# Score chunks of the first head inside the last context tiles of a perceiver layer

## The reference, cut to what matters

```python
q = (x @ wq).reshape(B, L, 16, 128)
k, v = ((x @ w).reshape(B, L, 4, 128) for w in (wk, wv))
k_ctx, v_ctx = ((h_ctx_kv @ w).reshape(B, T, 4, 128) for w in (wk_ctx, wv_ctx))
q, k, k_ctx = rms_norm(q, q_norm_w), rms_norm(k, k_norm_w), rms_norm(k_ctx, k_norm_w)
q, k = rope(q), rope(k)
k_full, v_full = concatenate([k_ctx, k]), concatenate([v_ctx, v])   # T + L = 4352 keys
scores = einsum('blhd,bmhd->bhlm', q, repeat(k_full, 4)) * scale + mask   # own keys causal
out = einsum('bhlm,bmhd->blhd', softmax(scores), repeat(v_full, 4)) @ wo
```

## Time and profile before

| | us |
|---|---|
| median of 3 runs | 1052.37 (1051.82 to 1052.49) |
| profiled execution | 1051.38 |
| its span, first to last instruction | 1049.3 |

### The profile page before, as it was taken

How to read it: one execution, slowest core, us unless ns; L and a number is a source line. 1 busy time by engine, 2 the same in 40 slices (tenths; PEclk the granted TensorE clock), 3 DMA queues, 4 the chain that set the end, 5 groups by cost and what they waited for, 6 DMA issues and landing times.

```text
span 1049.3 us, 15552 instructions
## 1 busy us (share of the span) xinstructions
PE 1035.7 (99%) x5789; PEld 885.7 (84%) x5789; DVE 777.2 (74%) x1661; ACT 602.7 (57%) x1090; POOL 182.4 (17%) x200
## 2 busy tenths in 40 slices
PE   7999999999999999999999999999999999999998
PEld 6888888887888888888888888888886888888887
DVE  5856777648777777777877777877668877777775
ACT  4344434334865566665566666568448466666664
POOL 4643344330000000000000000002202112222221
PEclk9999999999999999999999999999999999999999
DMA  6658675498004240042200431004450376555540
GB/s 235 233 195 286 229 241 173 133 317 293 37 1 139 73 131 1 1 171 81 91 1 1 171 121 56 1 1 182 161 231 1 121 285 214 195 191 183 190 169 21
DMA packets 64155, 145.76 MB, mean 139 GB/s; under 512 B 3888, under 2 KB 42704, under 8 KB 62672
## 3 DMA queue, kind: packets, MB, share of 16 engines
q1 hardware_dynamic: 64080, 144.77, 40.0%
HBM read 108.55 MB, written 36.21 MB: 138 GB/s over the span
## 4 chain that ended last, share of the span: by engine, by line
PE 95%; DVE 2%; ACT 1%; POOL 0%; issue 0%; DMA 0%; ACTq 0%
PE bank L549 18%; PE bank L486 16%; PE bank L592 12%; PE bank L569 11%; PE bank L467 11%; PE bank L847 8%; PE bank L594 6%; PE bank L849 4%; PE bank L649 2%; PE bank L662 1%; PE bank L496 1%; PE bank L780 1%; PE bank L717 1%; DVE e_hl L1192 0%; PE bank L818 0%; PE bank L521 0%
## 5 line engine op out<-in xcount | busy, mean ns | idle before, releaser
L1058 DVE TENSOR_TENSOR pT<-bank,pT 128x512 fp32r<-128x512 f32 x272 | 184.8, 689 | 103.3 <-ACT pT L1485 101.5
L1485 ACT CAST pT<-bank 128x512 fp32r<-128x512 f32 x272 | 156.1, 594 | 142.7 <-PE bank L569 139.5
L592 PE MATMUL bank<-pT,vN 128*128 128x512 f32 (+1 forms) x544 | 225.7, 422 | 0.0
L549 PE MATMUL bank<-kT,qT_hi 128*128 128x512 f32 (+2 forms) x576 | 214.5, 391 | 2.1 <-DVE scores L1002 2.1
L1002 DVE TENSOR_SCALAR_CACHE_REDUCE scores<-bank 128x512 f32<-128x512 f32 x256 | 172.8, 686 | 1.7
L569 PE MATMUL bank<-ident,scores 128*128 128x128 f32 x1072 | 161.3, 272 | 0.4 <-DVE pT L1058 0.3
L1456 ACT ACTIVATE scores<-scores,neg_max 128x1024 f32<-128x1024 f32 (+2 forms) x128 | 154.0, 1203 | 5.7 <-DVE neg_max L1014 5.7
L594 PE MATMUL bank<-pT,vN 128*128 128x256 f32 (+1 forms) x544 | 152.5, 280 | 0.0
L486 PE MATMUL bank<-w_ctx_hi,ctx_hl 128*128 128x512 f32 x512 | 146.0, 398 | 6.5 <-ACT ctx_hl L1365 6.5
L847 PE MATMUL bank<-fT_parts,e_hl 128*128 128x512 f32 x392 | 140.0, 395 | 0.1
L569 PEld LDWEIGHTS bank<-ident,scores 128*128 128x128 f32 x1072 | 127.2, 140 | 12.1 <-DVE pT L1058 1.2
(11 more groups left out here) (224 smaller groups left out, 1563.9 us busy)
## 6 DMA issues: line engine op xcount, KB each, us to landing
e_raw<-in_experts SPq DMA_DIRECT2D x51, 768.0 KB, 4.3
k_spill<-k_stage SPq DMA_DIRECT2D x16, 1024.0 KB, 4.5
v_spill<-v_stage SPq DMA_DIRECT2D x16, 1024.0 KB, 8.4
vN<-v_spill SPq DMA_DIRECT2D x16, 1024.0 KB, 5.2
kT<-k_spill SPq DMA_DIRECT2D x15, 1024.0 KB, 5.3
ctx_raw<-in_ctx SPq DMA_DIRECT2D x15, 512.0 KB, 4.3
w_raw<-in_w_qkv SPq DMA_DIRECT2D x6, 1024.0 KB, 5.0
wo_sb<-in_wo SPq DMA_DIRECT2D x4, 1024.0 KB, 9.5
```

Source lines behind the costliest of these rows:

```text
L549: done = e.matmul(bank[b][:, 0:n], qT[a][:, h, qt * P:(qt + 1) * P], kT[:, w, lo:lo + n], start=m == 0, stop=m == 2)
L592: e.matmul(halves[:, :, q0:L], vN[:, 0, kt, :], ring[:, :, i * L + q0:(i + 1) * L], start=kt == 0, stop=False)
L1058: e.tensor_tensor(ring[:, 1, :], bank[tb][:, :], ring[:, 0, :], ALU.subtract).then_inc(p_lo, 1)
L1485: e.copy(ring[:, 0, :], bank[tb][:, :]).then_inc(p_hi, 1)
```

## The change

- Nine chunks of head 0 move into the last three context tiles, three in each, behind the steps `k` = 0, 1, 2 of `project`, in banks 6 and 7. DVE evicts a tile's three ahead of its other work for the tile.
- Five chunks are left for `second`, in banks 0, 2, 6, 7, 0; three of them go ahead of the transpose of tile 31's keys.
- `ahead` has 4 chunks of head 1 in place of 8; the other 4 follow in the steps of head 0.
- In tile 31 ACT squares the projected keys before it copies the transposed keys of tile 30, and DVE forms the rest of tile 30's keys behind the sum of squares. DVE forms the rest of tile 31's values only after both maxima of head 0. It forms the rest of tile 31's keys behind two evictions.
- SP loads pieces 0, 1 and 2 of the values ahead of the last spill, once all tiles are projected.
- Regions s01 and v change places, so `front` lies over k and s01, and `back` over spare, v, s23 and pt; `chunk_max` moves to region keep.

```diff
+EARLY = 3
...
-        for i, c in enumerate(EARLY_CHUNKS):
-            self.add(0, 0, c, (0, 2, 6, 7)[i % 4])
-        self.first = list(range(len(self.chunks)))
-        for c in EARLY_CHUNKS:
-            self.add(0, 1, c)
-        self.second = list(range(len(self.first), len(self.chunks)))
+        for i, (qt, c) in enumerate([(qt, c) for qt in range(2) for c in EARLY_CHUNKS]):
+            self.add(0, qt, c, (6, 7)[i % 2] if i < EARLY * 3 else (0, 2, 6, 7)[(i - EARLY * 3) % 4])
+        self.first = {NT - EARLY + i: list(range(3 * i, 3 * i + 3)) for i in range(EARLY)}
+        self.second = list(range(3 * EARLY, len(self.chunks)))
...
-        for _ in range(8):
+        for _ in range(4):
             self.ahead.append(self.add(1, *ahead.pop(0)))
...
-        sizes = dict(keep=12288, k=34816, v=34816, spare=16096, s01=34816, s23=34816, pt=12288, q=32768)
+        sizes = dict(keep=12288, k=34816, s01=34816, spare=16096, v=34816, s23=34816, pt=12288, q=32768)
...
PE, project(i):
+                    if i in plan.first and k < KD - 1:
+                        in_turns([plan.first[i][k]], None)
...
PE, after the tiles:
-            for s in plan.first:
-                in_turns([s], None)
+            in_turns(plan.second[:3], None)
             turn(NT - 1)
-            for s in plan.second + plan.third + plan.ahead:
+            for s in plan.second[3:] + plan.third + plan.ahead:
                 in_turns([s], None)
...
DVE, in the loop over tiles:
+                if i in plan.first:
+                    for s in plan.first[i]:
+                        evict(s)
-                if i >= 1:
+                if 1 <= i < NT - 1:
                     rest_of_k(i - 1)
                 after(i)
...
DVE, after(i), in place of the rest of the values:
+                if i < NT - 1:
+                    rest_of_v(i)
+                else:
+                    rest_of_k(i - 1)
...
DVE, after the tiles:
-            for s in plan.first:
+            for s in plan.second[:2]:
                 evict(s)
             rest_of_k(NT - 1)
-            for s in plan.second:
+            for s in plan.second[2:]:
                 evict(s)
             for qt in range(2):
                 for s in plan.third[2 * qt:2 * qt + 2]:
                     evict(s)
                 maximum(0, qt)
+            rest_of_v(NT - 1)
             for s in plan.ahead:
                 evict(s)
...
ACT, in the loop over tiles:
-                if i >= 1:
+                if 1 <= i < NT - 1:
                     main_of_k(i - 1)
-                after(i)
+                squares_of_k(i)
+                if i == NT - 1:
+                    main_of_k(i - 1)
+                main_of_v(i)
...
SP:
             load_k(0, NPIECE - 2, (NPIECE - 2) * PIECE, TC - BATCH)
+
+            sp.wait_ge(ctx_proj, NT)
+            for p in (0, 1, 2):
+                wait_spilled(v_out, p)
+                load_v(0, p)
             spill(NBATCH - 1)
-            for p in (0, 1, 2, NPIECE - 1, NPIECE - 2):
+            for p in (NPIECE - 1, NPIECE - 2):
                 wait_spilled(v_out, p)
                 load_v(0, p)
```

More of the change, by code:

```diff
@@ L163, in before, with last_in @@
         return self.bank_history[bank][k - 1] if k else None
+    def last_in(self, bank):
+        return self.bank_history[bank][-1][1]
     def last_chunk(self, h):
@@ L232, in build_program @@
         gate_w = keep.take("gate_w", [KD, NE])
-        front = Region(nc, region["k"].base, region["k"].size + region["v"].size)
+        front = Region(nc, region["k"].base, region["k"].size + region["s01"].size)
         xn = Region(nc, front.base, 4096).take("xn", [TT, DM])
@@ L275, in build_program @@
         pT = [reg.take(f"pT{i}", [2, 512], F32R) for i, reg in enumerate([region["pt"]] * 3 + [sp_])]
-        chunk_max = [sp_.take(f"chunk_max{i}", [NCHK]) for i in range(4)]
+        chunk_max = [keep.take(f"chunk_max{i}", [NCHK]) for i in range(4)]
         row_max = [sp_.take(f"row_max{i}", [1]) for i in range(4)]
@@ L563, in turn_weights @@
                 else:
-                    pe.wait_ge(maxed, plan.first[3] + 1)
+                    pe.wait_ge(maxed, plan.last_in(7) + 1)
                 for i, (kt, qt) in enumerate([(kt, qt) for kt in (2 * kk, 2 * kk + 1) for qt in range(2)]):
@@ L581, in weigh @@
                     elif h == 1:
-                        pe.wait_ge(maxed, plan.first[6] + 1)
+                        pe.wait_ge(maxed, plan.last_in(6) + 1)
                     else:
@@ L622, in spread_sums @@
                 done.then_inc(spread, 1)
-            for s in plan.first:
-                in_turns([s], None)
+            for i in range(NT):
+                project(i)
+                if i == 1:
+                    pe.wait_ge(consts, 7)
+                    for tt in range(TT):
+                        pe.wait_ge(ln_out, tt + 1)
+                        turn_rows(tt, tt, xn)
+                if i >= 1:
+                    turn(i - 1)
+                n, half = step_of(i)
+                if 1 <= n <= NSTEP and half == 0:
+                    own_turn(n - 1)
+                if 0 <= n < NSTEP and half == 0:
+                    own_project(n)
+            in_turns(plan.second[:3], None)
             turn(NT - 1)
-            for s in plan.second + plan.third + plan.ahead:
+            for s in plan.second[3:] + plan.third + plan.ahead:
                 in_turns([s], None)
@@ L907, in rest_of_k, with rest_of_v @@
                                        op0=ALU.mult, op1=ALU.subtract).then_inc(ks_lo, 1)
+            def rest_of_v(i):
+                z, slot, s = i % 2, (i // BT) % 2, i % BT
+                dve.wait_ge(v_hi, i + 1)
+                e.tensor_tensor(v_stage[slot][:, :, 1, s, :], bank[2 + z][:, :].rearrange("p (g d) -> p g d", g=NKV), v_stage[slot][:, :, 0, s, :],
+                                ALU.subtract).then_inc(v_lo, 1)
             def after(i):
-                z, slot, s = i % 2, (i // BT) % 2, i % BT
+                z = i % 2
                 dve.wait_ge(ksq_done, i + 1)
@@ L914, in after @@
                 e.tensor_scalar(k_ssq[z][:, :], k_ssq[z][:, :], 1.0 / HD, 1e-6, ALU.mult, ALU.add).then_inc(kssq_done, 1)
-                dve.wait_ge(v_hi, i + 1)
-                e.tensor_tensor(v_stage[slot][:, :, 1, s, :], bank[2 + z][:, :].rearrange("p (g d) -> p g d", g=NKV), v_stage[slot][:, :, 0, s, :],
-                                ALU.subtract).then_inc(v_lo, 1)
+                if i < NT - 1:
+                    rest_of_v(i)
+                else:
+                    rest_of_k(i - 1)
                 dve.wait_ge(krs_done, i + 1)
@@ L962, in dve_program @@
                 e.tensor_tensor(w_ctx[1][:, k], w_ctx_raw[:, k], w_ctx[0][:, k], ALU.subtract).then_inc(wc_lo, 1)
[L963 to L972, removed]
-                if i >= 1:
-                    rest_of_k(i - 1)
-                after(i)
[L976 to L984, removed]
             def evict(s):
@@ L1038, in rest_of_wo @@
                     e.tensor_tensor(wo_lo[:, i, :], wo_sb[:, i, :], wo_hi[:, i, :], ALU.subtract).then_inc(wo_lo_d, 1)
-            for s in plan.first:
+            for i in range(NT):
+                if i == 0:
+                    dve.wait_ge(x_in, 16)
+                    for tt in range(TT):
+                        layernorm(tt, tt, xn)
+                if i == 1:
+                    for tt in range(TT):
+                        dve.wait_ge(xnT_hi, tt + 1)
+                        e.tensor_tensor(xnT[:, 1, :, tt * P:(tt + 1) * P], bank[6 + tt][:, :].rearrange("p (k t) -> p k t", k=KD),
+                                        xnT[:, 0, :, tt * P:(tt + 1) * P], ALU.subtract).then_inc(xnT_lo, 1)
+                if i in plan.first:
+                    for s in plan.first[i]:
+                        evict(s)
+                if 1 <= i < NT - 1:
+                    rest_of_k(i - 1)
+                after(i)
+                if i == 1:
+                    split_w(0)
+                n, half = step_of(i)
+                if half == 1 and n % TT == 0 and n >= 0:
+                    split_w(n // TT + 1)
+                if 1 <= n <= NSTEP and half == 0:
+                    own_split(n - 1)
+                if 0 <= n < NSTEP and half == 0:
+                    own_rotate(n)
+            for s in plan.second[:2]:
                 evict(s)
             rest_of_k(NT - 1)
-            for s in plan.second:
+            for s in plan.second[2:]:
                 evict(s)
@@ L1375, in main_of_k, with squares_of_k @@
                              scale=k_w[:, 0:1]).then_inc(ks_hi, 1)
-            def after(i):
-                b, s, z = i // BT, i % BT, i % 2
-                slot = b % 2
+            def squares_of_k(i):
+                z = i % 2
                 act.wait_ge(ctx_proj, i + 1)
@@ L1383, in after, with main_of_v @@
                 e.activation(k_sq[z][:, :], bank[z][:, :], ACT.Square).then_inc(ksq_done, 1)
+            def main_of_v(i):
```

(2 more changed lines are left out.)

## The result

| | before | changed |
|---|---|---|
| median, us | 1052.09 (1050.57 to 1052.49, 4 runs) | 1056.89 (1056.72 to 1057.82, 4 runs) |
| profiled execution's span, us | 1049.3 | 1055.0 |
| granted clock, mean | 1.000 | 0.997 |

The ratio is 1.0048 (1.0036 to 1.0059): 4.8 us slower by the medians, where 5.5 were forecast (a median of 1056.9, where 1057.9 was forecast). The two profiled executions are 5.5 us apart (1051.38 and 1056.89).

What follows compares the result with a forecast made beforehand. PE, busy 99% of the span, was taken to bound the kernel. New idle A 1.1, B 2.25, C 0.7 and D 4.7, in all 8.8, less 3.3 regained, gave +5.5 us: 1057.9 us, range 1053.0 to 1060.8.

Steps and rivals of the forecast that it cites:

- nine chunks in the tiles: Last three context tiles: moved score work costs nothing, DVE's gap hides the evictions; tile 31 ends at 242.3.
- A: End of tile 31: PE runs out of work and waits for the keys to transpose, 1.1 us idle.
- B: Late chunks: chunk 14 waits for DVE's queue to evict chunk 13 from the same bank 0, 2.25 us.
- C: Chunk 21: its bank 1 is evicted behind the late subtraction of tile 31's values, 0.7 us.
- D: Before chunk 25: ACT's first weights copy waits for the last v spill, delaying DVE's evictions and PE, 4.7 us.
- rival 1: Behind the 4.7 us stall: PE's clock falls, 2.7 us more, 1060.6 us; chance 0.16.
- regained: PE's waits of before return: 3.0 us between context tiles and head 0's weights, 0.3 behind steps without score work.
- the prediction's "nothing": Moved regions and chunk_max change addresses alone, so they cost or gain nothing.
- The forecast landings: DMA queue, in order of issue: last k spill lands at 258.8, last v spill at 262.1.
- rival 2: Last v spill doesn't queue behind the reads, lands at 259.4; D is 2.0, time 1055.2 us; chance 0.17.
- The 0.3 us at head 1's start: PE's loss to DVE behind head 0 steps without score work, counted as regained, else 0.
- Rival 4: Not slower: DVE never behind, 3.3 us regained, only 1.1 and 0.7 us of waiting left, 1050.9 us; chance 0.10.

Runs made afterwards that it cites:

- experiment 6: Changed kernel plus 11 matmuls of 512 columns, result unread, filling PE's wait before chunk 25; ratio 1.0035 to the kernel before.
- experiment 1: Changed kernel with the rest of tile 31's values subtracted directly behind that tile's norm; ratio 1.0048 to the kernel before.
- experiment 2: Changed kernel with the three pieces of values loaded behind the last spill again; ratio 1.0049 to the kernel before.
- experiment 3: Changed kernel with tile 31's values subtracted behind the norm and the three pieces of values loaded behind the last spill; ratio 1.0008 to the kernel before.
- experiment 5: Changed kernel with 8 chunks of head 1 ahead again in place of 4, late spill left; ratio 1.0009 to the kernel before.
- Experiment 8: Changed kernel with values subtracted early, loads behind the last spill, late chunks in banks 1, 2, 0, 1, eight ahead; 0.9985, rerun 0.9983, to the kernel before.
- experiment 4: Changed kernel with the late chunks in banks 1, 2, 0, 1 in place of 0, 1, 2, 0; ratio 1.0053 to the kernel before.

## Why the prediction was right

By its own steps, from the timelines of the changed kernel (a matmul of 512 columns taken as 0.23, of 256 as 0.12):

| step | forecast, us | profile |
|---|---|---|
| nine chunks in the tiles | 0 | 0; tile 31 ends at 242.2 (242.3) |
| A, keys of tile 31 | 1.1 | 1.06 (244.74 to 245.80) |
| B, chunk 14 in bank 0 | 2.25 | 2.33 (247.34 to 249.67) |
| slow matmuls behind B | not in it | 1.5 |
| C, chunk 21 | 0.7 | 0.4 |
| D, chunk 25 | 4.7 | 2.75 (260.69 to 263.44) |
| slow matmuls behind D | rival 1, 2.7 | 1.6 |
| regained | -3.3 | -3.0 |
| sum | +5.5 | +6.6 |

The sum of 6.6 fits the start of head 1's transposes, which moved from 281.66 to 288.36. The span grew by 5.7 only: 1.0 us comes back behind that point, 0.4 of it in the heads and the rest in the two blocks behind them, some hundredths at a time. Every kernel with the change's layout has it: from head 0's `rden` transposes to the last group of matmuls they take 764.0 to 764.1 us in ten of the eleven profiles, 764.4 in experiment 6 (with a wait of 0.4 us among the experts that no other has), and 765.0 in the one of the kernel before. The moved regions and `chunk_max` are what all of them share that reaches that far, so the prediction's "nothing" for these stands in doubt: -1.0 us is the likelier size. No kernel with the moved regions alone was run, and the cause stays open.

**Right.** The mechanism and its chain were those forecast, link by link: spill, ACT's copy, DVE's subtraction and eviction, chunk 25. The forecast landings were 258.8 and 262.1, the measured ones 258.7 and 261.35. Experiments 1 to 3 show the last v spill held twice over, by the late subtraction and by the queue, each enough alone, and experiment 5 that the four chunks taken from `ahead` were its cover. The order of landing, on which D rested against rival 2, was seen again in experiment 1: 12.7 us for a transfer that takes 8.2 with nothing ahead but its k spill. But in the changed kernel itself the queue added nothing that can be seen: the spill took 5.4 us behind the k spill, and 5.6 with an empty queue in experiment 2.

**Off.** Term D was mis-sized, 2.75 for 4.7: 0.7 since the spill landed earlier (2.65 behind the k spill, I took 3.3), and 1.3 since PE itself came to chunk 25 later than the forecast had it, held back by a slow stretch that I had not put behind B. There I argued from the 2.1 us wait of before, after which nothing was slow in the one profiled execution; that a wait of this length is always harmless does not follow from it (last section). Rival 1 came true in kind (slow matmuls behind the wait, shown by experiment 6), at 1.6 us and not 2.7; that D was shorter (by 2.0) and 3.1 us of slow matmuls were added partly cancel, and 1.0 us came back behind head 0. So the closeness of the forecast, 1057.9 for 1056.9, is in part luck: the chain was right, and three sizes were off in ways that offset each other. The 0.3 us at head 1's start was not regained: the wait is still on the list. Rival 2's price was wrong too: with an empty queue the spill takes 5.6, not 4.6, and experiment 2 was as slow as the change. Rival 4's 1050.9 us was reached by experiment 8 (1050.5), but with other orders, with 0.9 and 1.4 us of waiting left, and by the 1.0 us behind head 0 that it did not have.

## What to carry to other kernels

Before an operation is put off, follow its result to the last reader, through the DMA queue as well: here a subtraction of 0.7 us on DVE, put off to 255.25, kept ACT's copy from starting before 261.47. When two edits each delay the same thing, undoing one shows nothing; undo them together and one by one. And a wait that PE reaches with its buffer of other work used up costs more than its length where the clock falls with it: 1.5 to 1.6 us more each time here. A better time is not yet proof of its reason either: experiment 8 was faster, but not at the place where its gain was expected.

## What the runs showed of the hardware that I had not expected

- The clock fell around B in the profile of the changed kernel (0.9 us of waiting, then 2.2, with 1.5 us of work between) and in those of experiments 1, 2, 3, 5 and 6, with the same waits. It fell around D too, a single wait of 2.5 to 2.7 us behind at least 3 us of work without a wait (changed kernel, experiments 1 and 2). It stayed at 1.00 in the profiles with a single wait of 2.1 (before), with 0.9 and 1.3 (experiment 4), and with 0.9 and 1.4 (experiment 8).
- The same kernel can go either way. Of 63 executions of the kernel before that ran beside the experiments, 32 have a mean granted clock of 0.998, the value of the profiles with one slow stretch, and are on average 0.7 to 0.8 us longer than the 31 with 1.000 (1052.44 and 1051.77, 1052.21 and 1051.42, 1052.32 and 1051.51 on the three chips). In experiment 3 it is ten of eleven, in experiment 5 nine of eleven. All 22 executions of experiment 8's kernel, which has no wait above 1.4 us behind the first, have 1.000. So the wait of 2.1 us probably does cost the kernel before something in half of its executions; no profile shows such an execution, so where the clock fell in it is not shown.
- It does not fall at a fixed distance from the work. In the changed kernel it was about 1 us behind chunk 14's start (the slice from 250.5 to 251.0 has 0.77, those up to 254.0 have 0.50). In experiment 6 it fell ahead of chunk 14, which starts at 248.51, while PE stood idle. In experiment 4, with 4.4 us of waiting, it fell 2 us before chunk 25, and PE worked at 0.50 from 263.38 to 268. Experiment 6, then experiment 4:

```profile
248.00:248.50 0.50, 0.00 (x0) 0.02 (x1) 0.37 (x4) 0.00 (x0) 0.00 (x0) 0.82 0.99 410
...
261.00:263.00 2.00, 0.00 (x0) 0.00 (x0) 0.97 (x2) 1.59 (x3) 0.00 (x0) 0.56 0.36 64
```

- A v spill with an empty queue ahead took 5.6 us (experiment 2), a k spill of the same size 4.4 to 4.6. Pieces of values were issued 0.5 us behind the v spill; whether they or the v spill's own addresses make the difference was not tried.
